# ScalarE and VectorE take the work of a query/key head in another order

## The chip, the cores and the metric

The kernel runs on one core of one Trainium2 chip. The metric is the device time of one execution in microseconds (us). Matmuls run on TensorE (PE in the profile, its weight loads PEld); elementwise work runs on ScalarE (ACT), VectorE (DVE) and GpSimd (POOL); SyncE (SP) issues most transfers. The engines run their own lists of instructions in order and wait for each other by semaphores.

## What is computed

A layer on x of 32 x 32 x 512: a channel mix chosen by condition, attention with 32 heads of 128 over sequences of 32, then a state space convolution and a feed-forward product with low-rank additions. The change touches the attention's query/key part alone:

```python
q = hidden_states @ Wq + bq
k = hidden_states @ Wk + bk
q = rms_norm(q, gq)      # over all 4096 columns: sums of squares over all heads
k = rms_norm(k, gk)
attn = einsum('bhqd,bhkd->bhqk', q, k) * scale   # then softmax, times v, times Wo
```

The 1024 tokens are the moving side of the products. The norms are applied to the scores later, so the head loop only adds up the squares of q and k.

## The kernel before

Each fp32 product is made of three fast matmuls: both sides are split into a high part (rounded) and a low part (the rest), and hi*hi, hi*lo and lo*hi are added in PSUM (L636 to L638). For the weights ScalarE makes `w_hi` by a copy (`split_hi`, L915) and VectorE makes `w_lo` by a subtraction (`split_lo`, L1141).

Queries and keys of a head are made together by a fast scheme with seven half products, p1 to p7, instead of eight, each 128 x 512 with two chunks of depth, six matmuls. The sums and differences of weight blocks that it needs are made by GpSimd (`combine`, L422: four operations, two heads ahead and more), and the sums of products by VectorE (`post`, L1193: `c11`, `u2`, `u4`, `c12`, `c22`, `u3`, `c21`), which reads PSUM and the tile `qk_sb`.

Weights and `qk_sb` have two slots, by the parity of the head. The query/key stage runs from some 24 us to 441 us of the span. The lists of a head h are written out by hand:

- TensorE, `head_qk` (L673): wait for `w_lo` of h; p1, p2; wait for `c21` of h-1; p6, p5, p3, p7; scores of h-1 (`head_scores`, L662, which waits for the scaled query, `c21` and for the scores of h-2 to be extracted, s_ok); wait for `u2` of h; p4. Each product also waits for its PSUM bank.
- ScalarE, `head` (L973): split of the next head's weights, blocks 0 to 4 (L981); key eviction of p1 with bias (L985), which releases `c11`; split of blocks 4 to 7 (L987); square of the key of h-1 (L971, behind `c21`); wait for `c12`; square of the query of h (L1000); scale of the query (L1003); extraction of the scores of h-1 (`extract`, L960, four instructions).
- VectorE, `head` (L1234): `c21` of h-1; `split_lo` of h+1 (L1144); `c11`, `u2`, `u4`; addition of the key squares of h-1 (L1232); `c12`, `c22`, `u3`; addition of the query squares of h (L1232).
- SyncE: the load of the weights of h+3 waits for `split_lo` of h+1 (`wlo_ok`), and so does GpSimd's `combine`.

Behind the last head the value stage starts: SyncE loads the first value weights `wv_raw` when p4 of head 30 is done (L312), ScalarE (L1017) and VectorE (`split_v`, L1270) split them, and TensorE makes value group 0, then the scores of head 31 (L748 to L752). `wv_raw` lies where `w_raw` of slot 0 lay, `wv_hi` where `w_hi` and part of `w_lo` of slot 0 lay.

Of the kernel before, what the change touches and what calls it, by code (L numbers as in the profile page):

```python
# [22 lines left out]
F32 = mybir.dt.float32  # L23
F32R = mybir.dt.float32r
I32 = mybir.dt.int32
ALU = mybir.AluOpType
ACT = mybir.ActivationFunctionType
# [5 lines left out]
HEADS, HD = 32, 128  # L33
INNER = HEADS * HD
KC = FEAT // P
# [26 lines left out]
def build_program(nc, x, cond_idx, lengths, cond_w, wq, bq, wk, bk, wv, bv, wo, bo, gq, gk,  # L62
# [3 lines left out]
    with ctx:  # L66
# [129 lines left out]
        ws_start, ws_ok, whi_ok, wlo_ok = (sem(n) for n in ("ws_start", "ws_ok", "whi_ok", "wlo_ok"))  # L196
# [63 lines left out]
        def _(sp):  # L260
# [48 lines left out]
                sp.wait_ge(wo_mm, t * G)  # L309
                load_o(t, wo_raw)  # L310

            sp.wait_ge(p4_mm, HEADS - 1)  # L312
            load_v(0)
            sp.wait_ge(p4_mm, HEADS)
            load_o(0, wo_raw)
# [574 lines left out]
        def _(act):  # L890
# [24 lines left out]
            def split_hi(slot, lo, hi):  # L915

                return sc.activation(w_hi[slot][:, lo:hi, :].rearrange("p b n -> p (b n)"),  # L917
                                     w_raw[slot][:, lo + 1:hi + 1, :].rearrange("p b n -> p (b n)"), ACT.Copy)
# [10 lines left out]
            for g in range(4):  # L929
                mix_out(g)  # L930
            act.wait_ge(ws_start, 4)
            split_hi(0, 0, 7).then_inc(whi_ok, 2)
            for g in range(4, G):
                mix_out(g)
            act.wait_ge(prm_mm, 1)
# [17 lines left out]
            def extract(h):  # L953


                act.wait_ge(s_mm, h + 1)
                dst = scores[:].rearrange("p h g k -> p (h g k)")[:, bass.ds(here(h) * (G * 32), G * 32)]
                for b in range(BPG):
                    src = bank(6, 1024)[quadrant(b), :].rearrange("p (g k) -> p g k", g=G)[:, :, quadrant(b)]
                    last = sc.activation(dst[quadrant(b), :].rearrange("p (g k) -> p g k", g=G), src, ACT.Copy)  # L960
                last.then_inc(s_ok, 1)

            def square_k(h, slot):
                act.wait_ge(c21_ok, h + 1)
                if isinstance(h, int) and h == 0:
                    out = sumsq[:, 1, :]
                else:
                    out = sq[:, 1, :]
                    if not (isinstance(h, int) and h == 1):
                        act.wait_ge(k_sum, h - 1)  # L970
                sc.activation(out, qk_sb[:, slot, 1, :], ACT.Square).then_inc(k_sq, 1)  # L971

            def head(h, slot, last_head=False):  # L973
                first = isinstance(h, int) and h == 0
                if not last_head:
                    if first:
                        act.wait_ge(ws_start, 8)
                    else:
                        act.wait_ge(ws_ok, h * 4)
                        act.wait_ge(p4_mm, h)  # L980
                    split_hi(1 - slot, 0, 4).then_inc(whi_ok, 1)  # L981
                act.wait_ge(p1_mm, h + 1)
                if not (isinstance(h, int) and h < 2):
                    act.wait_ge(s_mm, h - 1)
                sc.activation(qk_sb[:, slot, 1, halves(0)], bank(0), ACT.Identity, bias=bias("bk", h)).then_inc(p1_ok, 1)  # L985
                if not last_head:
                    split_hi(1 - slot, 4, 7).then_inc(whi_ok, 1)  # L987
                if first:
                    for n in range(4):
                        t_hi_out(n)  # L990
                else:
                    square_k(h - 1, 1 - slot)
                act.wait_ge(c11_ok, h + 1)
                act.wait_ge(c12_ok, h + 1)
                if first:
                    sc.activation(sumsq[:, 0, :], qk_sb[:, slot, 0, :], ACT.Square).then_inc(q_sq, 1)
                else:
                    if not (isinstance(h, int) and h < 2):
                        act.wait_ge(q_sum, h - 1)
                    sc.activation(sq[:, 0, :], qk_sb[:, slot, 0, :], ACT.Square).then_inc(q_sq, 1)  # L1000
                act.wait_ge(q_sq, h + 1)
                at = here(h)
                sc.activation(qk_sb[:, slot, 0, :], qk_sb[:, slot, 0, :], ACT.Copy,  # L1003
                              scale=gqk[:, bass.ds(at, 1)]).then_inc(q_ok, 1)
                if not first:
                    extract(h - 1)

            act.wait_ge(gqk_ok, 2)
            head(0, 0)
# [1 line left out]
            with act.Fori(1, HEADS // 2 - 1) as i:  # L1011
                for j in range(2):
                    head(i * 2 + j, j)
            head(HEADS - 2, 0)
            head(HEADS - 1, 1, last_head=True)
            act.wait_ge(wv_in, 16)
            sc.activation(wv_hi[:].rearrange("p c n -> p (c n)"), wv_raw[:].rearrange("p c n -> p (c n)"),  # L1017
                          ACT.Copy).then_inc(wvhi_ok, 1)
            square_k(HEADS - 1, 1)


            def value_out(t, g):
# [94 lines left out]
        def _(dve):  # L1117
# [22 lines left out]

            def split_lo(h, slot):  # L1141

                dve.wait_ge(whi_ok, h * 2 + 2)
                v.tensor_tensor(w_lo[slot][:].rearrange("p b n -> p (b n)"),  # L1144
                                w_raw[slot][:, 1:8, :].rearrange("p b n -> p (b n)"),
                                w_hi[slot][:].rearrange("p b n -> p (b n)").bitcast(F32), ALU.subtract).then_inc(wlo_ok, 1)
# [79 lines left out]
            def add_squares(m, h, done, total):  # L1226


                dve.wait_ge(done, h + 1)
                if not (isinstance(h, int) and h == 1):  # L1230
                    dve.wait_ge(total, h - 1)
                v.tensor_tensor(sumsq[:, m, :], sumsq[:, m, :], sq[:, m, :], ALU.add).then_inc(total, 1)  # L1232

            def head(h, slot, last_head=False):  # L1234
                first = isinstance(h, int) and h == 0
                if not first:
                    post("c21", h - 1, 1 - slot)
                    if not last_head:
                        dve.wait_ge(p4_mm, h)
                if not last_head:  # L1240
                    split_lo(h + 1, 1 - slot)
                post("c11", h, slot)
                post("u2", h, slot)
                post("u4", h, slot)
                if not first:
                    if not (isinstance(h, int) and h == 1):
                        add_squares(1, h - 1, k_sq, k_sum)
                post("c12", h, slot)
                post("c22", h, slot)
                post("u3", h, slot)  # L1250
                if not first:
                    add_squares(0, h, q_sq, q_sum)

            dve.wait_ge(gqk_ok, 2)
            head(0, 0)
# [7 lines left out]
                    head(i * 2 + j, j)  # L1263
            head(HEADS - 2, 0)

            def split_v(t, parts=(0, 1, 2, 3)):
                if 0 in parts:
                    dve.wait_ge(wvhi_ok, t + 1)
                for c in parts:
                    last = v.tensor_tensor(wv_lo[:, c, :], wv_raw[:, c, :], wv_hi[:, c, :].bitcast(F32), ALU.subtract)  # L1270
                if KC - 1 in parts:
                    last.then_inc(wvlo_ok, 1)

            head(HEADS - 1, 1, last_head=True)
            split_v(0)
            post("c21", HEADS - 1, 1)
            add_squares(1, HEADS - 1, k_sq, k_sum)


# [175 lines left out]
```

## Time and profile before

| | us |
|---|---|
| median of 3 runs | 950.04 (949.18 to 950.06) |
| the profiled execution | 949.06 |
| its span | 947.3 |
| TensorE busy | 877.5 (93%) |
| VectorE busy | 600.8 (63%) |
| ScalarE busy | 384.4 (41%) |
| GpSimd busy | 438.2 (46%) |

"Busy" is the time in which an engine had an instruction under way. TensorE's matmuls are pipelined and their ends are modelled: one of 512 columns is shown with 0.39 us while the next starts 0.23 us after it. So TensorE's work is read from the starts. The granted clock is the share of full speed (2.4 GHz) that TensorE had; its other level is 1.2 GHz.

### The profile page before, as it was taken

Reading aid. Unit: us, or ns where it says so; the run is one execution under the profiler, and the core shown is the slowest. Engines: PE = TensorE matmul, PEld = TensorE weight load, DVE = VectorE, ACT = ScalarE, POOL = GpSimd, SP = SyncE. Lnnn points to the kernel's source line nnn. Section 1 sums busy time; section 2 is a strip of 40 time slices with the busy share of each in tenths; the row PEclk is TensorE's granted clock in tenths of the full one; section 3 lists DMA queues with packets and bytes.
Section 4 is the critical chain, followed back from the end, with each engine's and each line's share of the span. In section 5 each row is a group of like instructions: output and inputs, shape, how many; then the busy total and the mean of one; then the engine's idle time right before and its main releaser. Section 6 shows DMA issues by size and latency. Waiting matters only on the chain.

```text
span 947.3 us, 12406 instructions
## 1 busy us (share of the span) xinstructions
PE 877.5 (93%) x4529; PEld 722.6 (76%) x4529; DVE 600.8 (63%) x650; ACT 384.4 (41%) x523; POOL 438.2 (46%) x401
## 2 busy tenths in 40 slices
PE   5698799999999999997889989999999999999998
PEld 4586588777777777776678868888888888888466
DVE  5974977777777777774775634677666765534431
ACT  3454455555555555554342342314142323222410
POOL 0888822223333333303999433699639990000500
PEclk9898999999999999998989989999999999999999
DMA  5142111111111111102001112411141111157402
GB/s 161 45 129 53 44 44 44 44 44 37 31 43 44 44 44 44 44 15 74 19 27 45 45 31 65 38 48 41 44 90 45 45 45 47 71 195 199 124 12 78
DMA packets 83570, 56.51 MB, mean 60 GB/s; under 512 B 33639, under 2 KB 66759, under 8 KB 83415
## 3 DMA queue, kind: packets, MB, share of 16 engines
q1 hardware_dynamic: 82576, 55.67, 20.3%
q10 hardware_dynamic: 966, 0.48, 0.2%
q8 instruction: 17, 0.28, 0.1%
q14 instruction: 11, 0.08, 0.0%
HBM read 52.32 MB, written 3.82 MB: 59 GB/s over the span
## 4 chain that ended last, share of the span: by engine, by line
PE 49%; ACT 3%; DVE 2%; issue 1%; DMA 1%; ACTq 0%; DVEq 0%
PE psum L590 13%; PE psum L591 13%; PE psum L592 13%; PE psum L729 5%; PE psum L833 1%; PE psum L862 1%; PE psum L884 1%; DMA wv_raw<-in_wv 1%; DVE wv_lo L1270 1%; PE psum L845 0%; PE psum L787 0%; ACT x2p L1098 0%; PE psum L805 0%; DVE wv_lo L1351 0%; ACT ang L1070 0%
## 5 line engine op out<-in xcount | busy, mean ns | idle before, releaser
L636 PE MATMUL psum<-t_hi,w_hi 128*128 128x512 f32 x256 | 107.6, 420 | 36.2 <-DVE qk_sb L1224 20.9
L1144 DVE TENSOR_TENSOR w_lo<-w_raw,w_hi 128x1792 fp32r<-128x1792 f32 x32 | 66.9, 2091 | 103.6 <-ACT w_hi L917 103.6
L430 POOL TENSOR_TENSOR w_raw<-w_raw 128x256 f32<-128x256 f32 x30 | 25.3, 842 | 199.5 <-DMA w_raw<-in_wk 199.3
L590 PE MATMUL psum<-wv_hi,mix_hi 128*128 128x512 f32 x256 | 102.6, 401 | 8.0 <-DVE wv_lo L1270 5.1
L637 PE MATMUL psum<-t_lo,w_hi 128*128 128x512 f32 x256 | 102.0, 398 | 0.0
L638 PE MATMUL psum<-t_hi,w_lo 128*128 128x512 f32 x256 | 101.6, 397 | 0.0
L591 PE MATMUL psum<-wv_lo,mix_hi 128*128 128x512 f32 x256 | 101.5, 397 | 0.0
L1360 DVE TENSOR_TENSOR acc<-psum,acc 128x512 f32<-128x512 f32 x64 | 44.2, 690 | 90.4 <-PE psum L592 90.2
L592 PE MATMUL psum<-wv_hi,mix_lo 128*128 128x512 f32 x256 | 101.4, 396 | 0.0
L1000 ACT ACTIVATE sq<-qk_sb 128x1024 f32<-128x1024 f32 x31 | 32.9, 1063 | 158.4 <-issue 154.3
L636 PEld LDWEIGHTS psum<-t_hi,w_hi 128*128 128x128 f32 x256 | 49.2, 192 | 56.1 <-DVE qk_sb L1224 31.0
L1036 ACT ACTIVATE attn_hi<-psum,params 128x512 fp32r<-128x512 f32 x64 | 43.7, 688 | 112.3 <-PE psum L729 111.8
L590 PE MATMUL psum<-wo_hi,attn_hi 128*128 128x512 f32 x224 | 87.4, 390 | 0.0
L591 PE MATMUL psum<-wo_lo,attn_hi 128*128 128x512 f32 x224 | 87.4, 390 | 0.0
L592 PE MATMUL psum<-wo_hi,attn_lo 128*128 128x512 f32 x224 | 87.2, 389 | 0.0
L1024 ACT ACTIVATE v_sb<-psum 128x512 f32<-128x512 f32 x64 | 38.1, 598 | 111.9 <-PE psum L592 111.4
L1232 DVE TENSOR_TENSOR sumsq<-sumsq,sq 128x1024 f32<-128x1024 f32 x62 | 80.2, 1294 | 1.1 <-ACT sq L971 1.1
L636 PE MATMUL psum<-mix_hi,w_hi 128*128 128x512 f32 x192 | 75.6, 394 | 1.7 <-ACT params L936 1.7
L637 PE MATMUL psum<-mix_lo,w_hi 128*128 128x512 f32 x192 | 75.4, 393 | 0.0
L638 PE MATMUL psum<-mix_hi,w_lo 128*128 128x512 f32 x192 | 75.2, 392 | 0.0
L729 PE MATMUL psum<-p_blocks,v_sb 128*128 128x128 f32 x512 | 60.8, 281 | 6.4 <-DVE p_blocks L1330 5.4
L917 ACT ACTIVATE w_hi<-w_raw 128x1024 fp32r<-128x1024 f32 (+2 forms) x63 | 60.5, 960 | 14.3 <-POOL w_raw L435 8.7
(233 smaller groups left out, 1958.0 us busy)
## 6 DMA issues: line engine op xcount, KB each, us to landing
w_raw<-in_wq SPq DMA_DIRECT2D x32, 256.0 KB, 2.9
w_raw<-in_wk SPq DMA_DIRECT2D x32, 256.0 KB, 3.2
wv_raw<-in_wv SPq DMA_DIRECT2D x8, 1024.0 KB, 5.4
toep<-kpad_dram SPq DMA_DIRECT2D x2, 4096.0 KB, 15.3
wo_raw<-in_wo SPq DMA_DIRECT2D x7, 1024.0 KB, 5.3
x_nat<-in_x SPq DMA_DIRECT2D x4, 512.0 KB, 5.9
acc<-in_x SPq DMA_DIRECT2D x1, 2048.0 KB, 10.0
out_dram<-o_stage SPq DMA_DIRECT2D x8, 256.0 KB, 2.0
```

Source lines behind the costliest of these rows:

```text
L590: mm(out, lh, rh, start=(n == 0), stop=False)
L591: mm(out, lh, rl, start=False, stop=False)
L592: last = mm(out, ll, rh, start=False, stop=(close and n == len(terms) - 1))
L636: mm(bank(n), wh, hi[:, c, tok], start=(i == 0), stop=False)
L637: mm(bank(n), wh, lo[:, c, tok], start=False, stop=False)
L638: last = mm(bank(n), wl, hi[:, c, tok], start=False, stop=(i == 1))
L729: last = mm(bank(2 + u % 4)[:, P * (g % 4):P * (g % 4) + P], v_sb[:, g, HD * h:HD * h + HD], p_blocks[:, h, g, :], start=True, stop=True)
L917: return sc.activation(w_hi[slot][:, lo:hi, :].rearrange("p b n -> p (b n)"), w_raw[slot][:, lo + 1:hi + 1, :].rearrange("p b n -> p (b n) ...
L1036: sc.activation(attn_hi[:, h, HALF * half:HALF * half + HALF], bank(2 + u % 4), ACT.Identity, bias=params[:, PARAM["bv"], bass.ds(at, 1)]) ...
L1144: v.tensor_tensor(w_lo[slot][:].rearrange("p b n -> p (b n)"), w_raw[slot][:, 1:8, :].rearrange("p b n -> p (b n)"), w_hi[slot][:].rearran ...
L1232: v.tensor_tensor(sumsq[:, m, :], sumsq[:, m, :], sq[:, m, :], ALU.add).then_inc(total, 1)
L1360: v.tensor_tensor(acc[:, g, :], bank(6 + g % 2), acc[:, g, :], ALU.add).then_inc(acc_ok, 1)
```

## The change

The lists of a head are put in another order on two engines.

- ScalarE: the split of the next head's weights becomes one instruction (blocks 0 to 7) and stands behind the square of the key of h-1, ahead of the wait for `c11` and `c12`. The extraction of the scores of h-2 stands at the head of head h's list, where the extraction of h-1 had stood at the end of h's list; the last one, extract(HEADS - 2), stands behind the last square. In the last head the split of `wv_raw` stands where the weights' split stands in the others, behind a wait for p4 of head 30.
- VectorE: the addition of query squares of h-1 stands behind `c21` of h-1; `split_lo` of h+1 stands behind `c12` of h; in the last head `split_v(0)` stands there.
- `whi_ok` counts one a head instead of two.
- SyncE: the load of `wv_raw` waits for `split_lo` of head 30 instead of p4 of head 30.

The diff, without the two places where `split_v` only moves in the text and the initial count of `whi_ok`:

```diff
@@ -309,7 +309,7 @@
                 sp.wait_ge(wo_mm, t * G)
                 load_o(t, wo_raw)
 
-            sp.wait_ge(p4_mm, HEADS - 1)
+            sp.wait_ge(wlo_ok, HEADS - 1)
             load_v(0)
             sp.wait_ge(p4_mm, HEADS)
             load_o(0, wo_raw)
@@ -970,26 +970,37 @@
                         act.wait_ge(k_sum, h - 1)
                 sc.activation(out, qk_sb[:, slot, 1, :], ACT.Square).then_inc(k_sq, 1)
 
+            def split_next(h, slot):
+
+                if isinstance(h, int) and h == 0:
+                    act.wait_ge(ws_start, 8)
+                else:
+                    act.wait_ge(ws_ok, h * 4)
+                    act.wait_ge(p4_mm, h)
+                split_hi(1 - slot, 0, 7).then_inc(whi_ok, 1)
+
+            def split_v0():
+
+                act.wait_ge(wv_in, 16)
+                act.wait_ge(p4_mm, HEADS - 1)
+                sc.activation(wv_hi[:].rearrange("p c n -> p (c n)"), wv_raw[:].rearrange("p c n -> p (c n)"),
+                              ACT.Copy).then_inc(wvhi_ok, 1)
+
             def head(h, slot, last_head=False):
                 first = isinstance(h, int) and h == 0
-                if not last_head:
-                    if first:
-                        act.wait_ge(ws_start, 8)
-                    else:
-                        act.wait_ge(ws_ok, h * 4)
-                        act.wait_ge(p4_mm, h)
-                    split_hi(1 - slot, 0, 4).then_inc(whi_ok, 1)
+                if not (isinstance(h, int) and h < 2):
+                    extract(h - 2)
                 act.wait_ge(p1_mm, h + 1)
-                if not (isinstance(h, int) and h < 2):
-                    act.wait_ge(s_mm, h - 1)
                 sc.activation(qk_sb[:, slot, 1, halves(0)], bank(0), ACT.Identity, bias=bias("bk", h)).then_inc(p1_ok, 1)
-                if not last_head:
-                    split_hi(1 - slot, 4, 7).then_inc(whi_ok, 1)
                 if first:
                     for n in range(4):
                         t_hi_out(n)
                 else:
                     square_k(h - 1, 1 - slot)
+                if last_head:
+                    split_v0()
+                else:
+                    split_next(h, slot)
                 act.wait_ge(c11_ok, h + 1)
                 act.wait_ge(c12_ok, h + 1)
                 if first:
@@ -1002,8 +1013,6 @@
                 at = here(h)
                 sc.activation(qk_sb[:, slot, 0, :], qk_sb[:, slot, 0, :], ACT.Copy,
                               scale=gqk[:, bass.ds(at, 1)]).then_inc(q_ok, 1)
-                if not first:
-                    extract(h - 1)
 
             act.wait_ge(gqk_ok, 2)
             head(0, 0)
@@ -1013,10 +1022,8 @@
                     head(i * 2 + j, j)
             head(HEADS - 2, 0)
             head(HEADS - 1, 1, last_head=True)
-            act.wait_ge(wv_in, 16)
-            sc.activation(wv_hi[:].rearrange("p c n -> p (c n)"), wv_raw[:].rearrange("p c n -> p (c n)"),
-                          ACT.Copy).then_inc(wvhi_ok, 1)
             square_k(HEADS - 1, 1)
+            extract(HEADS - 2)
 
 
             def value_out(t, g):
@@ -1140,7 +1147,7 @@
 
             def split_lo(h, slot):
 
-                dve.wait_ge(whi_ok, h * 2 + 2)
+                dve.wait_ge(whi_ok, h + 1)
                 v.tensor_tensor(w_lo[slot][:].rearrange("p b n -> p (b n)"),
                                 w_raw[slot][:, 1:8, :].rearrange("p b n -> p (b n)"),
                                 w_hi[slot][:].rearrange("p b n -> p (b n)").bitcast(F32), ALU.subtract).then_inc(wlo_ok, 1)
@@ -1231,14 +1238,20 @@
                     dve.wait_ge(total, h - 1)
                 v.tensor_tensor(sumsq[:, m, :], sumsq[:, m, :], sq[:, m, :], ALU.add).then_inc(total, 1)
 
...
             def head(h, slot, last_head=False):
                 first = isinstance(h, int) and h == 0
                 if not first:
                     post("c21", h - 1, 1 - slot)
-                    if not last_head:
-                        dve.wait_ge(p4_mm, h)
-                if not last_head:
-                    split_lo(h + 1, 1 - slot)
+                    if not (isinstance(h, int) and h == 1):
+                        add_squares(0, h - 1, q_sq, q_sum)
                 post("c11", h, slot)
                 post("u2", h, slot)
                 post("u4", h, slot)
@@ -1246,10 +1259,14 @@
                     if not (isinstance(h, int) and h == 1):
                         add_squares(1, h - 1, k_sq, k_sum)
                 post("c12", h, slot)
+                if last_head:
+                    split_v(0)
+                else:
+                    if not first:
+                        dve.wait_ge(p4_mm, h)
+                    split_lo(h + 1, 1 - slot)
                 post("c22", h, slot)
                 post("u3", h, slot)
-                if not first:
-                    add_squares(0, h, q_sq, q_sum)
 
             dve.wait_ge(gqk_ok, 2)
             head(0, 0)
@@ -1263,17 +1280,9 @@
                     head(i * 2 + j, j)
             head(HEADS - 2, 0)
 
...
             head(HEADS - 1, 1, last_head=True)
-            split_v(0)
             post("c21", HEADS - 1, 1)
+            add_squares(0, HEADS - 1, q_sq, q_sum)
             add_squares(1, HEADS - 1, k_sq, k_sum)
 
 
```

## Rows read from the trace of the kernel before

**Rows 1.** TensorE waits, whole span: us in total, times, longest.

```profile
PE psum L636 <- DVE qk_sb L1224: 20.9, 24, 4.3
PE psum L636 <- DVE qk_sb L1205: 7.9, 3, 4.6
...
PE psum L590 <- DVE wv_lo L1270: 5.1, 1, 5.1
```

**Rows 2.** Timeline, ScalarE, one head: start us, us, operation, idle before.

```profile
201.12 1.06 ACT L1000 ACTIVATE sq<-qk_sb 128x1024 f32<-128x1024 f32 x1 [5.10 <-issue]
202.34 1.15 ACT L1003 ACTIVATE qk_sb<-qk_sb,gqk 128x1024 f32<-128x1024 f32 x1
203.39 1.52 ACT L960 ACTIVATE scores<-psum 32x256 f32 x4
204.94 1.06 ACT L917 ACTIVATE w_hi<-w_raw 128x1024 fp32r<-128x1024 f32 x1
206.02 0.69 ACT L985 ACTIVATE qk_sb<-psum,params 128x512 f32<-128x512 f32 x1
...
207.34 1.05 ACT L971 ACTIVATE sq<-qk_sb 128x1024 f32<-128x1024 f32 x1
213.49 1.06 ACT L1000 ACTIVATE sq<-qk_sb 128x1024 f32<-128x1024 f32 x1 [5.10 <-issue]
```

**Rows 3.** Timeline, VectorE, the same head.

```profile
207.48 2.02 DVE L1144 TENSOR_TENSOR w_lo<-w_raw,w_hi 128x1792 fp32r<-128x1792 f32 x1 [3.21 <-ACT w_hi L917]
209.42 0.75 DVE L1201 SCALAR_TENSOR_TENSOR qk_sb<-psum,dqk,qk_sb 128x512 f32<-128x512 f32 x1
...
211.53 1.22 DVE L1232 TENSOR_TENSOR sumsq<-sumsq,sq 128x1024 f32<-128x1024 f32 x1
212.67 0.74 DVE L1213 SCALAR_TENSOR_TENSOR qk_sb<-psum,dqk,qk_sb 128x512 f32<-128x512 f32 x1
213.44 0.69 DVE L1217 TENSOR_TENSOR qk_sb<-psum,qk_sb 128x512 f32<-128x512 f32 x1
...
214.65 1.31 DVE L1232 TENSOR_TENSOR sumsq<-sumsq,sq 128x1024 f32<-128x1024 f32 x1
```

**Rows 4.** Timeline, TensorE, head 1: p1, its scores, the next p1.

```profile
43.98 0.40 PE L636 MATMUL psum<-mix_hi,w_hi 128*128 128x512 f32 x1
...
52.16 0.38 PE L669 MATMUL psum<-qk_sb 128*128 128x128 f32 x2
...
55.32 0.39 PE L636 MATMUL psum<-mix_hi,w_hi 128*128 128x512 f32 x1
```

**Rows 5.** Timeline, TensorE, VectorE: p1 (heads 6, 31) and a c21.

```profile
117.58 0.39 PE L636 MATMUL psum<-mix_hi,w_hi 128*128 128x512 f32 x1
...
117.85 0.69 DVE L1224 TENSOR_TENSOR qk_sb<-psum,qk_sb 128x512 f32<-128x512 f32 x1 [0.74 <-PE psum L638]
...
423.25 0.39 PE L636 MATMUL psum<-mix_hi,w_hi 128*128 128x512 f32 x1
```

**Rows 6.** Busy time by stretch, value stage: engines, granted clock, DMA share, GB/s.

```profile
600.00:700.00 100.00, 100.00 (x553) 85.61 (x552) 65.03 (x60) 27.73 (x37) 75.85 (x32) 1.00 0.21 53
```

**Rows 7.** Timeline, GpSimd and VectorE, start of the stage.

```profile
90.64 4.60 POOL L458 TENSOR_TENSOR acc<-acc,bo_rows 128x2048 f32<-128x2048 f32 x1
...
93.25 3.86 DVE L1144 TENSOR_TENSOR w_lo<-w_raw,w_hi 128x1792 fp32r<-128x1792 f32 x1 [6.34 <-ACT w_hi L917]
...
102.28 4.27 DVE L1232 TENSOR_TENSOR sumsq<-sumsq,sq 128x1024 f32<-128x1024 f32 x1
```

**Rows 8.** Timeline, TensorE, first value group and the scores behind it.

```profile
440.90 0.77 PE L590 MATMUL psum<-wv_hi,mix_hi 128*128 128x512 f32 x1 [5.08 <-DVE wv_lo L1270]
...
446.05 1.95 PE L669 MATMUL psum<-qk_sb 128*128 128x128 f32 x16
```

**Rows 9.** Page, transfers (KB each, us to landing); timeline, ScalarE, value split.

```profile
wv_raw<-in_wv SPq DMA_DIRECT2D x8, 1024.0 KB, 5.4
...
436.31 1.91 ACT L1017 ACTIVATE wv_hi<-wv_raw 128x2048 fp32r<-128x2048 f32 x1
```

More of the change, by code:

```diff
@@ L931, in _ @@
             act.wait_ge(ws_start, 4)
-            split_hi(0, 0, 7).then_inc(whi_ok, 2)
+            split_hi(0, 0, 7).then_inc(whi_ok, 1)
             for g in range(4, G):
@@ L1232, in add_squares, with split_v @@
                 v.tensor_tensor(sumsq[:, m, :], sumsq[:, m, :], sq[:, m, :], ALU.add).then_inc(total, 1)
+            def split_v(t, parts=(0, 1, 2, 3)):
+                if 0 in parts:
+                    dve.wait_ge(wvhi_ok, t + 1)
+                for c in parts:
+                    last = v.tensor_tensor(wv_lo[:, c, :], wv_raw[:, c, :], wv_hi[:, c, :].bitcast(F32), ALU.subtract)
+                if KC - 1 in parts:
+                    last.then_inc(wvlo_ok, 1)
             def head(h, slot, last_head=False):
@@ L1264, in _ @@
             head(HEADS - 2, 0)
[L1266 to L1272, printed above, removed]
             head(HEADS - 1, 1, last_head=True)
-            split_v(0)
             post("c21", HEADS - 1, 1)
+            add_squares(0, HEADS - 1, q_sq, q_sum)
             add_squares(1, HEADS - 1, k_sq, k_sum)
```

## Prediction

> **What bounds the kernel now.** I read the list of waits first, for TensorE: of its long idle times the largest total, 20.9 us in 24 pieces, ends with L1224, which is VectorE's `c21` of the query/key stage; another 7.9 us in 3 pieces ends with L1205, VectorE's `u2`, and 5.1 us with the first `wv_lo` at L1270 [rows 1]. TensorE has 93% of the span as busy time, so the question is what makes it wait in the heads.
>
> Then I read the timeline of one head on ScalarE and VectorE. ScalarE squares a query at 201.12 and the next one at 213.49: 12.37 us a head [rows 2]. Between them stands a closed ring in which each piece starts as the one before ends: square 201.12, scale 202.34, score extraction 203.39, first part of the weight split 204.94, key eviction (L985) 206.02 with the second part of the split behind it, VectorE's `split_lo` 207.48, `c11`, `u2`, `u4` from 209.42, the addition of key squares 211.53, `c12` 212.67, and again the square at 213.49 [rows 2, 3]. In this ring TensorE has no part.
>
> TensorE's own need is seen in head 1, where it did not wait: p1 starts at 43.98 and p1 of the next head at 55.32, so 11.34 us [rows 4]. The seven products take (52.16 - 43.98) / 6 = 1.36 us each for the six ahead of the scores, and scores with p4 take 55.32 - 52.16 = 3.16. So the stage is bound by the ring of the two other engines, and TensorE spends the difference of about 1.03 us a head on the wait ahead of p6. From p1 of head 6 (117.58) to p1 of head 31 (423.25) there are 25 heads in 305.67 us, 12.23 each; the first few of them still used up a lead [rows 5].
>
> **The change, part by part.** No arithmetic goes away; one ScalarE instruction a head does (two pieces of the split become one). The 1024-column piece takes 1.06 us [rows 2], so 1792 columns take at most 1.06 x 1.75 = 1.86 (an estimate).
>
> *The ring.* The weight split leaves the place ahead of L985, `split_lo` leaves the place ahead of `c11`, and the squares of the query are added behind `c21` and not ahead of it. The extraction moves in the text only: extract(h-1) at the head of the next head's list still follows the scale of head h at once. What is left of the ring: square 1.22, scale 1.05, extraction 1.55, L985 0.69, `c11`/`u2`/`u4` 2.11, key squares 1.14, `c12` 0.82 [rows 2, 3]. Sum 8.6 us, under 11.34. TensorE becomes the bound if nothing else is late, so I lay out a head of 11.34 with p1 at 0. A product's result is seen by VectorE 0.27 us behind the start of the next product (`c21` at 117.85, p1 at 117.58) [rows 5].
>
> VectorE: `c21` of the old head waits for p4, so from 0.27 and 0.69 long, then the query squares, 1.31, which end at about 2.2. `c11` waits for p2: 2.73 + 0.27 = 3.0. `u2` follows p6 at 4.4, `u4` follows p5 at 5.7, key squares 6.4 to 7.5, `c12` to 8.3, `split_lo` 2.02 to 10.3, then `c22` and `u3` (0.77 and 0.61, from the spacing 212.67, 213.44 and 214.65) to 11.7 [rows 3]. The next `c21` starts at 11.7 instead of 11.6 and ends at 12.4, where p6 needs it at 11.34 + 2.73 = 14.1. The new wait that matters is that p1 of the next head needs `split_lo`: ready at 10.3, wanted at 11.34, so 1.0 us of room where there had been some 4. VectorE is busy some 9 us a head, and its list has about 0.8 us of room before `c11`.
>
> ScalarE: L985 waits for p1 and starts at about 1.6, the key square (1.05) ends at 3.3, the whole split at 5.2, in time for 8.3. The query square follows `c12` at 8.3, the scale ends at 10.7, and the extraction, whose scores ended at 10.1, at 12.2, that is 0.9 of the next head, ahead of L985 at 1.6. All other semaphores of TensorE are early: scores(h-1) wants the scale and s_ok at 8.2 and has them at about -0.6 and 0.9. Queued behind `split_lo`'s wait on VectorE are `c22` and `u3`, needed by p7 and p6 only a head later.
>
> SyncE's loads of weights hang on `split_lo`, which is now late in a head; the load and GpSimd's sums for head h+3 are wanted three heads later by the split, so a load (some 3 us) and the sums (some 4) are hidden with two heads to spare. If that cover were gone, the whole of about 7 us would fall on each head.
>
> So 25 heads take 283.5 in place of 305.67: **22.2 us**. TensorE without a pause at full clock for 100 us is seen in the value stage, granted clock 1.00 [rows 6], so I charge no throttling.
>
> *The start of the stage (up to p1 of head 6).* Here GpSimd is late: between its weight sums it works on exponentials and adds the bias rows to `acc` (L458). The sums for head 5 are done when L458 starts, 90.64 [rows 7]. The split ends at 92.5, and `split_lo`, which had taken 3.86 us from 93.25 in place of 2.02, ends where it ended before, 97.1, because L458 runs until 95.24 [rows 7]. The row shows it: the two never run together. The Trainium skill, SBUF — State Buffer, section Who interferes with whom, says that an operation of VectorE with two inputs in SBUF and one of GpSimd that reads SBUF hold a common read port in turns, each to its end; the trace agrees (3.86 against 2.02). Without that rule p1 of head 5 would come at 94.5 and the sum would gain 2.6 us more.
>
> p1 of head 5 is then at 97.2 and p1 of head 6 at 108.5, or when `split_lo`(6) is done: key squares had ended at 102.28 + 4.27 = 106.55 behind the same GpSimd operation [rows 7], then `c12` and `split_lo`, 2.9, so 109.4. TensorE idles for some 6 us ahead of 97.2, and after such idle times it ran at half clock: the value group at 440.90 took 5.15 us until 446.05, where twelve matmuls take 2.73, a loss of 2.4 [rows 8]. I charge it: 108.5 + 2.4 = 110.9. Gain 117.58 - 110.9 = **6.7 us**, bounds 5 (if half clock lasts longer) and 8.2 (if it doesn't come).
>
> *The end of the stage.* The load of `wv_raw` waits for `split_lo`(30) in place of p4(30): about 12 us earlier, with a landing of 5.4 us [rows 9]. Its split takes 1.91 on ScalarE [rows 9] and is behind the key square: 3.3 to 5.2 of head 31, and VectorE's half (about 2.5) ends at 10.8, before p4 ends. So the value group starts 11.34 behind p1(31), where it was 440.90 - 423.25 = 17.65: **6.3 us**. Its half clock goes with the idle time: **2.4 us**. Against it stands extract(30), now behind the last key square: `c21`(31) ends at 12.3, key square 13.4, extraction 14.9; the last scores want it at 14.1 with the value group done: **-1.0 us** (0 to -1.6).
>
> *Behind it* the same chains (norm, softmax, GpSimd's tables) start from the same points and move as a whole; 0, with 2 either way.
>
> Sum: 22.2 + 6.7 + 6.3 + 2.4 - 1.0 = 36.6 us. The profiled execution took 949.06 (span 947.3 with 1.8 around it), 0.1% under the median of 950.04. 949.06 - 36.6 = **912.5 us**, -3.9%.
>
> **The rivals.**
> *A. A second ring takes over part of it.* p1(h) to `c12`(h) to `split_lo`(h+1) to p1(h+1) closes at 10.3. If operations of both engines lengthen each other (a blocked `split_lo` took 3.86, so +1.84 [rows 7]), it closes at 12.1 and 25 heads give nothing more than 3 us. For it: VectorE has two more pairs of SBUF inputs in a row. Against it: GpSimd's sums start some 3.8 us behind the end of `split_lo`, when VectorE works from PSUM. Half of that, 11.2, costs nothing; the full amount gives 912.5 + 19 = 932.
> *B. Slower than before.* The same gate, one mechanism: `split_lo` waits behind `c12`, so each head's first product hangs on the end of the VectorE list. It costs more than the whole gain if the ring closes above 12.23 + 14.4 / 25 = 12.8 us, 2.5 over what I count, as when blocking (1.84) meets each head together with a late `u4`. At 13.2 the time is 949.06 + 10 = 959.
> *C. It doesn't do what it says:* the room is used up by another wait and TensorE's idle time only moves from p6 to p1. Then the stage keeps 12.23, only the end gains its 7.7 and the start perhaps 1: 940. For no change at all, both must be lost too.
> *D. The clock.* The Trainium skill, TensorE: Matmul & The Clock Gate, section HAM oscillation, says that idle gaps throttle the array. By rows, one more stretch of half clock costs 2.4 us or somewhat more: 915 to 917. It stays in the forecast's own range.
>
> **How the numbers follow.** Forecast with D 0.80 (906 to 920), A 0.10 (920 to 935), C 0.05 (935 to 948), no difference 0.02, B 0.03. Four fifths are held by 906 to 922: the lower end takes the start and the end at their best and a shorter head (11.3), the upper end some of A. A measurement of this kernel tells 0.2% from no change. Faster 0.95, same 0.02, slower 0.03.
>
> **What would show it.** The square L1000 every 11.3 us instead of 12.37; no TensorE wait on L1224 in the middle heads; `split_lo` behind `c12`, ending about 1 us ahead of p1; the value group directly behind p4(31), and a wait of 1 us ahead of the last scores, ended by the extraction; `split_lo` near 97 us still long. It is wrong if TensorE's waits reappear ended by L1144.

## The result and the profile after

| | before | after |
|---|---|---|
| median of 4 executions, us | 949.63 | 912.9 (912.25 to 914.61) |
| the profiled execution | 949.06 | 912.63 |
| its span | 947.3 | 910.8 |
| TensorE busy | 877.5 (93%) | 865.6 (95%) |
| VectorE busy | 600.8 (63%) | 592.7 (65%) |
| ScalarE busy | 384.4 (41%) | 378.3 (42%) |
| GpSimd busy | 438.2 (46%) | 418.8 (46%) |

The ratio is 0.9616, with a 95% interval of 0.9599 to 0.9633: 36.7 us less by the medians, 36.5 by the spans of the two profiled executions.

The waits of TensorE over the whole span of the changed kernel, as in [rows 1]: us in total, times, longest.

```profile
PE psum L636 <- DVE w_lo L1151: 10.1, 3, 6.1
...
PE psum L729 <- DVE p_blocks L1339: 4.5, 1, 4.5
...
PE psum L669 <- ACT scores L960: 1.0, 1, 1.0
```

The 24 waits on `c21` are gone, and so are those on `u2` and on the first `wv_lo`. New are three on `split_lo` (now L1151), all at the start of the stage (1.6, 2.4 and 6.1 us, ahead of p1 of heads 1, 4 and 5), and one of 1.0 us on the extraction of scores.

One head on ScalarE in the changed kernel, the same view as [rows 2]:

```profile
201.25 1.06 ACT L1011 ACTIVATE sq<-qk_sb 128x1024 f32<-128x1024 f32 x1 [3.37 <-issue]
202.46 1.15 ACT L1014 ACTIVATE qk_sb<-qk_sb,gqk 128x1024 f32<-128x1024 f32 x1
203.51 1.52 ACT L960 ACTIVATE scores<-psum 32x256 f32 x4
205.97 0.69 ACT L994 ACTIVATE qk_sb<-psum,params 128x512 f32<-128x512 f32 x1 [0.94 <-PE psum L638]
206.56 1.05 ACT L971 ACTIVATE sq<-qk_sb 128x1024 f32<-128x1024 f32 x1
207.51 1.69 ACT L917 ACTIVATE w_hi<-w_raw 128x1792 fp32r<-128x1792 f32 x1
212.57 1.06 ACT L1011 ACTIVATE sq<-qk_sb 128x1024 f32<-128x1024 f32 x1 [3.37 <-issue]
```

From square to square it is 11.32 us, not 12.37. The key eviction (now L994) no longer starts where the piece ahead of it ends: it waits 0.94 us for TensorE's p1. The ring is open.

The same head on VectorE, as [rows 3]:

```profile
204.56 0.69 DVE L1231 TENSOR_TENSOR qk_sb<-psum,qk_sb 128x512 f32<-128x512 f32 x1 [0.26 <-PE psum L638]
205.17 1.22 DVE L1239 TENSOR_TENSOR sumsq<-sumsq,sq 128x1024 f32<-128x1024 f32 x1
207.38 0.75 DVE L1208 SCALAR_TENSOR_TENSOR qk_sb<-psum,dqk,qk_sb 128x512 f32<-128x512 f32 x1 [0.99 <-PE psum L638]
208.64 0.69 DVE L1212 TENSOR_TENSOR qk_sb<-psum,qk_sb 128x512 f32<-128x512 f32 x1 [0.51 <-PE psum L638]
210.00 0.69 DVE L1216 TENSOR_TENSOR qk_sb<-psum,qk_sb 128x512 f32<-128x512 f32 x1 [0.67 <-PE psum L638]
210.61 1.22 DVE L1239 TENSOR_TENSOR sumsq<-sumsq,sq 128x1024 f32<-128x1024 f32 x1
211.74 0.74 DVE L1220 SCALAR_TENSOR_TENSOR qk_sb<-psum,dqk,qk_sb 128x512 f32<-128x512 f32 x1
212.40 2.02 DVE L1151 TENSOR_TENSOR w_lo<-w_raw,w_hi 128x1792 fp32r<-128x1792 f32 x1
```

`c21`, `c11`, `u2` and `u4` now each wait for TensorE, 0.26 to 0.99 us. Behind `u4` key squares, `c12` and `split_lo` stand back to back until 214.42, and TensorE starts the next p1 at 215.61:

```profile
113.73 0.39 PE L636 MATMUL psum<-mix_hi,w_hi 128*128 128x512 f32 x1
...
204.29 0.39 PE L636 MATMUL psum<-mix_hi,w_hi 128*128 128x512 f32 x1
...
215.61 0.39 PE L636 MATMUL psum<-mix_hi,w_hi 128*128 128x512 f32 x1
...
396.73 0.39 PE L636 MATMUL psum<-mix_hi,w_hi 128*128 128x512 f32 x1
```

These are p1 of heads 6, 14, 15 and 31. From head 6 to head 31 it is 283.00 us, where it was 305.67 [rows 5]: 11.32 a head. The busy time by stretch over these 25 heads, before (PE, PEld, VectorE, ScalarE, GpSimd; granted clock; DMA share; GB/s):

```profile
117.60:423.20 305.60, 289.75 (x1451) 240.02 (x1450) 221.33 (x247) 172.99 (x246) 86.77 (x93) 1.00 0.13 39
```

and after:

```profile
113.70:396.70 283.00, 283.00 (x1451) 241.81 (x1450) 222.56 (x251) 171.33 (x228) 70.23 (x96) 1.00 0.16 48
```

1451 matmuls in both and a full clock in both; after, TensorE is busy all of the 283.00 us.

### The profile page after: what moved, and what is told of

Same layout as the page of the kernel before. It is cut to its first block, busy times and chain, and to the rows that moved or that the text cites. A ratio compares the mean times of both kernels' runs of the same rounds, so it can differ in the third digit from the quotient of the medians.

```text
span 910.8 us, 12373 instructions
## 1 busy us (share of the span) xinstructions
PE 865.6 (95%) x4529; PEld 721.2 (79%) x4529; DVE 592.7 (65%) x650; ACT 378.3 (42%) x492; POOL 418.8 (46%) x401
## 4 chain that ended last, share of the span: by engine, by line
PE 85%; POOL 4%; DVE 4%; ACT 3%; DMA 1%; issue 1%; ACTq 0%; SPq 0%; POOLq 0%; DVEq 0%
PE psum L590 13%; PE psum L591 13%; PE psum L592 13%; PE psum L636 10%; PE psum L637 10%; PE psum L638 10%; PE psum L729 6%; PE psum L669 5%; PE psum L833 2%; PE psum L862 1%; DVE w_lo L1151 1%; PE psum L884 1%; PE psum L612 1%; POOL small L450 1%; DMA wv_raw<-in_wv 1%
## 5 line engine op out<-in xcount | busy, mean ns | idle before, releaser
L636 PE MATMUL psum<-t_hi,w_hi 128*128 128x512 f32 x256 | 103.5, 404 | 7.3 <-DVE t_lo L1197 7.3
L1239 DVE TENSOR_TENSOR sumsq<-sumsq,sq 128x1024 f32<-128x1024 f32 x62 | 76.3, 1231 | 0.0
L1151 DVE TENSOR_TENSOR w_lo<-w_raw,w_hi 128x1792 fp32r<-128x1792 f32 x32 | 67.1, 2097 | 8.9 <-ACT w_hi L917 8.9
L729 PEld LDWEIGHTS psum<-p_blocks,v_sb 128*128 128x128 f32 x512 | 60.9, 199 | 5.8 <-issue 4.9
L669 PEld LDWEIGHTS psum<-qk_sb 128*128 128x128 f32 x512 | 62.0, 191 | 3.8 <-issue 1.4
## 6 DMA issues: line engine op xcount, KB each, us to landing
acc<-in_x SPq DMA_DIRECT2D x1, 2048.0 KB, 10.7
```

Source lines behind the costliest of these rows:

```text
L636: mm(bank(n), wh, hi[:, c, tok], start=(i == 0), stop=False)
L669: last = mm(bank(6, 1024)[:, P * g:P * g + P], qk_sb[:, slot, 0, P * g:P * g + P], qk_sb[:, slot, 1, P * g:P * g + P], start=True, stop=True)
L729: last = mm(bank(2 + u % 4)[:, P * (g % 4):P * (g % 4) + P], v_sb[:, g, HD * h:HD * h + HD], p_blocks[:, h, g, :], start=True, stop=True)
```

## The experiments

Each is an edit of the changed kernel and was run several times beside the kernel before. The kernel before had a median of 949.2 to 949.4 us there. The changed kernel was run once more among the last ones:

> The changed kernel itself on the same chip as the three others: 913, ratio 0.9616 to the kernel before, and a half-clock stretch more or less (1.7 us each) as the spread between its executions.

Measured: 912.96 us (ratio 0.9617, 0.9601 to 0.9633). Against it the medians below are read; 0.2% of it is 1.8 us.

### Which of the moves opens the ring

**ScalarE's split back in two pieces and in the old places** (`split_next` then splits blocks 0 to 4 only, and `whi_ok` counts two a head again; not shown):

```diff
                 if not (isinstance(h, int) and h < 2):
                     extract(h - 2)
+                if not last_head:
+                    split_next(h, slot)
                 act.wait_ge(p1_mm, h + 1)
                 sc.activation(... bank(0), ACT.Identity, bias=bias("bk", h)).then_inc(p1_ok, 1)
+                if not last_head:
+                    split_hi(1 - slot, 4, 7).then_inc(whi_ok, 1)
...
-                else:
-                    split_next(h, slot)
```

> The changed kernel with the weight split of ScalarE back in its two old pieces and places (blocks 0 to 4 ahead of the key eviction, 4 to 7 behind it). Theory V (VectorE's order alone opens the ring): the ring from c12 to c12 then holds square 1.22, scale 1.05, extraction 1.55, split 1.08, eviction 0.6, c11 to u4 2.11, key squares 1.14, c12 0.82, sum 9.6 us, under TensorE's 11.32; time 913, within 0.3% of the changed kernel. Rival S (ScalarE's order carries the gain): the key eviction is late again, the heads go back to 12.2 us or more, time 935 to 945.

Measured: 914.35 us, ratio 0.9631 (0.9615 to 0.9647), p1 to p1 of 11.32 us in all middle heads. ScalarE's order carries 1.4 us at most, which a measurement hardly tells from nothing. By the traces it is nothing: p1 of head 31 starts at 397.38, against 397.48 in the changed kernel run again, and 1.5 us more lie at the very end (95.9 us from the last wait on `wv_lo` on, not 94.4, with a granted clock of 0.96 and not 0.98).

**`split_lo` back ahead of `c11`, ScalarE as changed:**

```diff
+                if not last_head:
+                    if not first:
+                        dve.wait_ge(p4_mm, h)
+                    split_lo(h + 1, 1 - slot)
                 post("c11", h, slot)
...
                 post("c12", h, slot)
                 if last_head:
                     split_v(0)
-                else:
-                    if not first:
-                        dve.wait_ge(p4_mm, h)
-                    split_lo(h + 1, 1 - slot)
```

> The changed kernel with split_lo back ahead of c11, ScalarE as changed. Theory V: the ring closes over both splits and the key square as well: 1.22 + 1.05 + 1.55 + 0.60 + 0.95 + 1.61 + 1.94 + 2.11 + 1.14 + 0.82 = 13.0 us a head, slower than the kernel before in the heads; 25 x 1.7 = 42 us more than the changed kernel, 950 to 960. Rival S: ScalarE's order keeps most of the gain, under 930.

Measured: 959.75 us, ratio 1.0114 (1.0096 to 1.0132): 47 us over the changed kernel and slower than the kernel before; heads of 13.07 to 13.11. ScalarE and VectorE in one head of it, the split and what stands behind it:

```profile
199.60 1.69 ACT L917 ACTIVATE w_hi<-w_raw 128x1792 fp32r<-128x1792 f32 x1
207.34 1.06 ACT L1011 ACTIVATE sq<-qk_sb 128x1024 f32<-128x1024 f32 x1 [6.04 <-issue]
```

```profile
201.32 2.02 DVE L1151 TENSOR_TENSOR w_lo<-w_raw,w_hi 128x1792 fp32r<-128x1792 f32 x1 [3.85 <-ACT w_hi L917]
203.27 0.74 DVE L1208 SCALAR_TENSOR_TENSOR qk_sb<-psum,dqk,qk_sb 128x512 f32<-128x512 f32 x1
```

`split_lo` waits 3.85 us for the whole split, which itself stands behind the key square now, and the chain goes on over `c11` to the query square at 207.34. ScalarE's half of the change without the move of `split_lo` is a loss, though this kernel keeps the query squares and the end of the stage as changed; VectorE's half without ScalarE's, again with the end as changed, gives all but 1.4 us of the gain.

**The query squares back ahead of `c21`:** `add_squares(0, h, ...)` stands behind `u3` again.

> The changed kernel with the addition of the query squares back in its old place (behind u3, ahead of c21). By the measured offsets c21 would then end some 1.2 us later, at 2.1 us behind p4 in place of 0.95, where p6 needs it at 2.73: no change, 913, heads of 11.32. Rival (c21 behind the additions was the wait that TensorE stood in): waits on c21 ahead of p6 return, 0.3 us or more a head, 920 and above.

Measured: 915.3 us, ratio 0.9644 (0.9628 to 0.966). The heads stay at 11.32, so this wait was none of TensorE's as long as the ring is open. Of the 2.3 us, 1.0 is seen at the end of the stage: the scores of head 31 wait 1.99 us for the extraction, not 0.99, as `c21` and the last key square are later. Another 1.2 is TensorE's clock: behind the wait of 2.90 us at 525.09 the granted clock of the 12 us from 524 on is 0.72, where it is 0.86 in the changed kernel, and the stretch from there to the next wait takes 293.65 us, not 292.4. No run moves `split_lo` and nothing else; that the other two moves are not needed is shown for each by itself, here and above.

**All orders inside the heads as before, the change around the last head kept** (the three edits together):

> Both engines' orders inside the heads as before (two split pieces, split_lo ahead of c11, query squares ahead of c21); kept is only the change around the last head: value weights loaded behind split_lo(30), their split inside head 31, extract(30) behind the last key square. My sum gives this part 6.3 + 2.4 - 1.0 = 7.7 us: 942, heads of 12.3. Rival: the end gives nothing of its own, 949; or more, if what followed the value group also gained from it, 939.

Measured: 942.18 us (seven executions, 939.16 to 946.90), ratio 0.9929 (0.9902 to 0.9956), heads of 12.2 to 12.5. By the medians the end is worth 7.2 us by itself, 7.7 by the sum; the interval allows 4 to 9. The steps agree less well than the totals: the first value group starts 12.4 us behind p1 of head 31, so 5.2 of the 6.3 are there; it takes 4.87 us until the last scores, where it took 5.15, so 0.3 of the 1.4, as the scores wait 1.99 us for the extraction; and 1.0 more comes behind them, where I had put 0.

**The load of the first value weights behind p4(30) again:**

```diff
-            sp.wait_ge(wlo_ok, HEADS - 1)
+            sp.wait_ge(p4_mm, HEADS - 1)
             load_v(0)
```

> The changed kernel with the load of the first value weights waiting for p4 of head 30 again, the rest as changed. p4(30) ends at about 397 of the changed kernel's span; issue 0.4 and landing 5.5 bring the weights at 402.8, ScalarE's split 1.9 ends at 404.7, and VectorE reaches its half at 404.84 anyway. Theory O (the order around the last head carries the 6.3 us, the earlier load nothing): 913, within 0.3% of the changed kernel. Rival L (the earlier load carries it): the value group starts 5 us later and at half clock, 918 to 921.

Measured: 912.98 us, ratio 0.9625 (0.9599 to 0.9651), value group 11.32 behind p1(31). The earlier load gives nothing; the place of the value split in the lists does it.

### How much room the new gate has

`split_lo` now stands right ahead of the first product that needs it. To measure the room, part of `w_lo` is worked out twice, ahead of the full `split_lo`, in one kernel 768 columns and in the other all 1792:

```diff
                 dve.wait_ge(whi_ok, h + 1)
+                v.tensor_tensor(w_lo[slot][:, 0:3, :]..., w_raw[slot][:, 1:4, :]...,
+                                w_hi[slot][:, 0:3, :]..., ALU.subtract).then_inc(again, 1)
+                dve.wait_ge(again, h + 1)
                 v.tensor_tensor(w_lo[slot][:]..., w_raw[slot][:, 1:8, :]..., w_hi[slot][:]..., ALU.subtract)
```

> The changed kernel with 768 columns of w_lo worked out twice, ahead of each split_lo: about 0.87 us more on VectorE behind c12 (by 2.02 us for 1792 columns). The room behind split_lo is 215.61 - 214.42 = 1.2 us in the changed kernel, so the heads stay at 11.32 and the time at 913 to 916. Rival (the gate of split_lo has no real room, since blocking by GpSimd uses it up): heads of 11.6 and more, 921 and above.

Measured: 925.24 us, ratio 0.9742 (0.9726 to 0.9758), heads of 11.65 to 11.80. This I had wrong: the room is smaller than I read it. One head of this kernel on GpSimd, VectorE and TensorE:

```profile
252.81 0.73 POOL L436 TENSOR_TENSOR w_raw<-w_raw 128x256 f32<-128x256 f32 x1
```

```profile
252.41 0.69 DVE L1221 TENSOR_TENSOR qk_sb<-psum,qk_sb 128x512 f32<-128x512 f32 x1 [0.67 <-PE psum L639]
253.02 1.60 DVE L1244 TENSOR_TENSOR sumsq<-sumsq,sq 128x1024 f32<-128x1024 f32 x1
254.55 0.74 DVE L1225 SCALAR_TENSOR_TENSOR qk_sb<-psum,dqk,qk_sb 128x512 f32<-128x512 f32 x1
255.21 0.94 DVE L1152 TENSOR_TENSOR w_lo<-w_raw,w_hi 128x768 fp32r<-128x768 f32 x1
256.18 2.02 DVE L1156 TENSOR_TENSOR w_lo<-w_raw,w_hi 128x1792 fp32r<-128x1792 f32 x1
```

```profile
258.26 0.50 PE L637 MATMUL psum<-mix_hi,w_hi 128*128 128x512 f32 x1
```

From `u4` to the end of `split_lo` it is 258.20 - 252.41 = 5.79 us; in the changed kernel 214.42 - 210.00 = 4.42. Of the 1.37 more, 0.97 is the added operation. The other 0.4 is the key squares: 1.60 us, not 1.22. GpSimd's last sum (252.81, 0.73) is still under way when they start at 253.02. The load of weights hangs on `split_lo`, the sums on the load, so a later `split_lo` pushes the sums into the key squares. In the changed kernel they miss each other by 0.5 us. From p1 to `u4` it is 5.84 us in this head (5.71 in the changed kernel), and from the end of `split_lo` to p1 0.06: together 11.69, the head as measured.

> The changed kernel with all 1792 columns of w_lo worked out twice: 1.93 us more. Behind the room of 1.2 us, 0.75 us a head are left over: heads of 12.1, 25 x 0.75 = 19 us, with the others some 21 to 24 more, 933 to 938, and TensorE's idle time ends with split_lo ahead of p1. Rival (VectorE's list is short of time as a whole and not by this gate): heads of 11.3 still, as VectorE's busy time of 9.1 + 1.9 = 11.0 us is under 11.32; 914.

Measured: 960.52 us, ratio 1.0114 (1.0092 to 1.0135), over 20 us above my range: heads of 12.62 to 12.88, not 12.1, with TensorE waiting 1.1 to 1.2 us for `split_lo` ahead of each p1. The wait ends where I said. The 2.0 added and the 0.4 of blocking (key squares of 1.53 and 1.59 us here as well), less a room of 1.0, make 1.4 a head, as measured. VectorE's list is not full; it is the gate. The time is 11 us above the kernel before at heads of 12.7, where rival B had put the turning point at 12.8: it had left out that the start loses as well (p1 of head 6 at 126.10, 12 us later than in the changed kernel).

### The start of the stage, and a faster version

**GpSimd's sums of heads 4 to 9 each stand two heads earlier in its list:**

```diff
             combine(3, 1, 64)
+            combine(4, 0, 96)
             exp_in_place(sm("ea"), sm("t0"), sm("t1"))
+            combine(5, 1, 96)
...
-            combine(4, 0, 96)
+            combine(6, 0, 128)
             exp_in_place(sm("ex"), sm("t0"), sm("t1"))
-            combine(5, 1, 96)
+            combine(7, 1, 128)
...
             for n in range(2):
+                combine(8 + n, n, 160)
                 gp.tensor_tensor(acc[:, 4 * n:4 * n + 4, :], ...).then_inc(acc_set, 1)
-                combine(6 + n, n, 128)
-            with pool.Fori(4, HEADS // 2) as i:
+            with pool.Fori(5, HEADS // 2) as i:
```

> The changed kernel with GpSimd's list put in another order at the start of the stage: the weight sums of heads 4 to 9 each stand two heads earlier against the exponentials and the bias additions to acc, which come later. Theory G (the start is bound by GpSimd's late sums, 2.4 + 6.1 us of idle TensorE ahead of p1 of heads 4 and 5 and 2.6 us of half clock behind them): 912.9 - 9 to 11 = 902 to 904. Rival (the idle time only moves, since the exponentials then meet the sums of the later heads): 908 to 913.

Measured: 907.31 us (903.53 to 911.84), ratio 0.9557 (0.9516 to 0.9598). p1 of head 6 is at 100.97, 12.8 us earlier, but ahead of p1 of head 8 a new wait of 5.57 us stands, with half clock behind it. GpSimd, VectorE and TensorE there:

```profile
122.92 4.52 POOL L461 TENSOR_TENSOR acc<-acc,bo_rows 128x2048 f32<-128x2048 f32 x1
```

```profile
122.94 6.38 DVE L1153 TENSOR_TENSOR w_lo<-w_raw,w_hi 128x1792 fp32r<-128x1792 f32 x1
```

```profile
129.38 0.80 PE L638 MATMUL psum<-mix_hi,w_hi 128*128 128x512 f32 x1 [5.57 <-DVE w_lo L1153]
```

`split_lo` starts 0.02 us behind a bias addition of 4.52 us and takes 6.38: that length and its own 1.9. The time lies between the two ranges, and the rival held in part: the time of the sums was won, and some of it was lost again, to the long additions and not to the exponentials as the rival had it.

**The same, with the two bias additions cut into eight, one behind the sums of each of heads 8 to 15** (the lines taken out, and VectorE's wait for eight of `acc_set` and not two, are not shown):

```diff
+            for g in range(G):
+                combine(8 + g, g % 2, (8 + g) // 2 * 32 + 32)
+                gp.tensor_tensor(acc[:, g, :], acc[:, g, :], bo_rows[:], ALU.add).then_inc(acc_set, 1)
+            with pool.Fori(8, HEADS // 2) as i:
```

> GpSimd's sums first, as before, and the two bias additions of 4.6 us each as eight of some 1.2 us, one behind each of the sums of heads 8 to 15. Theory P (one long GpSimd operation with SBUF inputs holds up split_lo for its whole length, 6.38 us where it takes 2.02): the idle time of 5.57 us ahead of p1 of head 8 and the half clock behind it go, heads of 11.32 from head 1 on, p1(31) at 384; 908.1 - 8.3 = 900. Rival: the pieces block split_lo or the key squares in eight heads by up to 1.2 us each, past the room of 1.0: 902 to 906.

Measured: 900.83 us (900.62 to 901.39), ratio 0.9491 (0.9475 to 0.9507). Heads of 11.32 to 11.45 from head 1 on, p1(31) at 385.46, and no wait of TensorE within them. This is the fastest version, 12.1 us under the changed kernel and 5.1% under the kernel before: 5.6 us by the sums moved forward, 6.5 by the pieces.

**extract(30) ahead of the last key square:** the two lines change places.

> The changed kernel with extract(30) ahead of the last key square and not behind it. The scores of head 31 waited 0.99 us for it at 411.92 (1.0 was my charge): it now ends at about 408.7, before the value group does at 410.8, so 1.0 us is gained: 912. Rival: the key square, 1.5 us later, makes the sums of squares late, nothing gained: 913.

Measured: 913.25 us, ratio 0.9631 (0.9612 to 0.965): nothing. The wait ahead of the last scores is gone, but not its microsecond. The waits of TensorE in this kernel, as above, and an operation that is longer, on VectorE, with GpSimd beside it:

```profile
PE psum L729 <- DVE p_blocks L1339: 5.7, 1, 5.7
PE psum L590 <- ACT v_sb L1031: 3.8, 2, 2.9
```

```profile
419.43 2.22 DVE L1296 SCALAR_TENSOR_TENSOR inv_norm<-var_k,var_q 128x256 f32<-128x256 f32 x1
```

```profile
418.58 2.78 POOL L479 TENSOR_TENSOR expo<-mult,small 128x1536 f32<-128x1536 f32 x1
```

The first `attend` waits 5.7 us for the softmax, not 4.5 (L1335, the scaling by `row_inv`, takes 2.36 us here and 1.23 in the changed kernel), and one value group 0.9 for an eviction. L1296 takes 2.22 us here and 0.97 in the changed kernel, and the traces say why: it ends 0.3 us behind GpSimd's L479 in both. L479 ends at 421.36 here and L1296 at 421.65; in the changed kernel L479 runs from 418.39 to 421.17 and L1296 from 420.48 to 421.45. In the kernel with both edits below it is the same again (409.63 and 409.91). GpSimd's list follows the last `c21`, which this edit doesn't move, so whatever reaches L1296 earlier waits there: the microsecond is lost to an operation of GpSimd.

> Both of the two: 1.0 us under the kernel with the pieces alone, 899. Rival as there.

Measured, both together: 902.77 us (899.38 to 903.85), ratio 0.9516 (0.95 to 0.9533), no better than the pieces alone. The profiled execution was the fastest of the four, at 899.38.

## Why the prediction was right, point by point

912.5 was forecast and 912.9 measured. The main term, the heads, is right for the reason given; that the total agrees to 0.4 us is luck, since the start gave 2.8 us too little and the part behind the stage 2.4 too much. By the steps of the sum, all from starts on TensorE (us):

| step | before | after | forecast | measured |
|---|---|---|---|---|
| up to p1 of head 6 | 117.58 | 113.73 | 6.7 | 3.9 |
| 25 heads, p1(6) to p1(31) | 305.67 | 283.00 | 22.2 | 22.7 |
| p1(31) to the first value group | 17.65 | 11.32 | 6.3 | 6.3 |
| value group to the last scores | 5.15 | 3.87 | 1.4 | 1.3 |
| from there to the end | 501.2 | 498.9 | 0 | 2.4 |
| sum | | | 36.6 | 36.5 |

**The heads and the ring.** Right in mechanism and in size. The ring of 12.37 was closed by `split_lo` ahead of `c11` (back there: 13.09, by its sum 13.0), and with it moved TensorE's own 11.32 is left. My sign of being wrong, waits of TensorE on this `split_lo`, did come, but in no middle head: only the three at the start. That only VectorE's place matters was my reading behind the result; the prediction had treated both moves together.

**The start.** Two terms miss and make up for each other, and this is the first: 6.7 was 2.8 too much, below my lower bound of 5. The step that failed is "the sums for head 5 are done when L458 starts, 90.64": I took GpSimd's list as it stood in the trace of before, and had called its loads and sums hidden. In the changed kernel, GpSimd (two views), VectorE and TensorE show:

```profile
49.02 0.74 POOL L430 TENSOR_TENSOR w_raw<-w_raw 128x256 f32<-128x256 f32 x1 [1.57 <-DMA w_raw<-in_wk]
...
53.59 2.17 POOL L411 TENSOR_SCALAR small<-small 128x32 f32<-128x32 f32 x1
...
74.77 1.73 POOL L431 TENSOR_TENSOR w_raw<-w_raw 128x256 f32<-128x256 f32 x1
...
93.24 4.51 POOL L458 TENSOR_TENSOR acc<-acc,bo_rows 128x2048 f32<-128x2048 f32 x1
```

```profile
53.59 2.02 DVE L1151 TENSOR_TENSOR w_lo<-w_raw,w_hi 128x1792 fp32r<-128x1792 f32 x1
...
95.04 4.59 DVE L1151 TENSOR_TENSOR w_lo<-w_raw,w_hi 128x1792 fp32r<-128x1792 f32 x1 [4.71 <-ACT w_hi L917]
```

```profile
81.95 0.50 PE L636 MATMUL psum<-mix_hi,w_hi 128*128 128x512 f32 x1 [2.41 <-DVE w_lo L1151]
...
99.69 0.79 PE L636 MATMUL psum<-mix_hi,w_hi 128*128 128x512 f32 x1 [6.12 <-DVE w_lo L1151]
```

The sums for head 5 are done at 93.24, 2.6 us later. At 53.59 a step of the exponential starts with `split_lo` and takes 2.17 us, where its like take 0.29; at 74.77 a sum takes 1.73, not 0.74. Each was held by an operation of VectorE with two inputs in SBUF that the new order had put beside it. But the kernel before has such pieces too, at other places, and the sum at 74.77 was not held there:

```profile
48.63 2.58 POOL L433 TENSOR_TENSOR w_raw<-w_raw 128x256 f32<-128x256 f32 x1
...
72.97 0.73 POOL L431 TENSOR_TENSOR w_raw<-w_raw 128x256 f32<-128x256 f32 x1
```

So the whole list has to be added up, from 39 us to the end of the sums for head 5. Before, eight operations are held, some 10.7 us together; after, nine, some 11.5. That is 0.8 of the 2.6 us. The list stands 0.3 later when this starts. The largest part, 1.57, is the wait at 49.02 for the weights of head 3: their load follows `split_lo` of head 1, which now stands behind `c12`, and is issued at 45.24 and not at 41.01.

So the hold-up that I charged in one direction (`split_lo` held by L458: here 4.59 us from 95.04) acts in the other as well. The idle time of 6.12 us and the half clock behind it (first matmul 0.79) came as charged.

**The end.** 6.3 by place of the value split, not by the earlier load, as the run with the late load shows. The half clock ahead of the last scores is gone, and the wait on the extraction came with 0.99 us where 1.0 was charged:

```profile
409.29 1.06 ACT L971 ACTIVATE sq<-qk_sb 128x1024 f32<-128x1024 f32 x1 [2.04 <-DVE qk_sb L1231]
410.26 1.52 ACT L960 ACTIVATE scores<-psum 32x256 f32<-32x256 f32 x4
```

```profile
408.05 0.39 PE L590 MATMUL psum<-wv_hi,mix_hi 128*128 128x512 f32 x1
...
411.92 0.80 PE L669 MATMUL psum<-qk_sb 128*128 128x128 f32 x5 [0.99 <-ACT scores L960]
```

The run with the extraction first shows that this wait is covered: without it the same time is spent at L1296, behind GpSimd's L479.

**Behind the stage.** I had said 0, 2 either way; it was 2.4, just outside. The reason I gave, that all chains behind the stage move as a whole, failed. By starts 0.8 us of it lie between the last scores and the first `attend` (29.92 before, 29.16 after), 0.2 from there to the next long wait, 1.3 from that to the one behind it (293.68 and 292.40), and 0.1 at the end. The 0.8 is on VectorE: its softmax chain meets GpSimd's tables at other points, and its scaling by `row_inv`, for one, takes 2.35 us before and 1.23 after. The 1.3 is TensorE's clock. Behind the same wait of 2.9 us for an eviction, at 559.21 before and 524.13 after, the stretches of 12 us read, before:

```profile
558.00:570.00 12.00, 10.79 (x35) 8.62 (x36) 8.43 (x8) 2.24 (x4) 9.83 (x28) 0.72 0.28 89
```

and after:

```profile
523.00:535.00 12.00, 10.87 (x41) 8.80 (x42) 9.10 (x9) 2.83 (x5) 9.83 (x28) 0.86 0.28 89
```

A granted clock of 0.72 is 2 x 0.28 x 12 = 6.7 us at 1.2 GHz, one of 0.86 is 3.4. Half of the difference would be 1.7 us saved; by the starts it is 1.3. The same wait stands ahead of both, so why it was shorter is open.

**The rivals.** A and B had the right mechanism with the wrong distance to it: the gate's room is 1.0 us, as laid out, but an operation that lengthens it also moves GpSimd's sums into the key squares, 0.4 more. The changed kernel is on the right side by little. C did not come. D is in the ledger with the one stretch charged and the one half as long.

## What to carry to other kernels

When the busiest engine stops a little in each turn of a loop, follow one turn from an instruction to itself on the other engines: if each piece starts as the one before ends and the sum is the period, take out of that ring the piece that nobody in it needs, and check which engine's list closes it, as here only one of two moves did the work. The moved piece has a new deadline; its room is to be read with what hangs on its end (the load, the sums, and which operations of other engines they then meet), not from its own length alone. And a gain ahead of a stage that is held by another engine's list is not read off that list as it was, since the list itself shifts with its neighbours and with the loads that hang on them.

## What the runs showed of the hardware that was not expected

One GpSimd operation with SBUF inputs holds up a VectorE operation with two SBUF inputs for its whole length: 6.38 us for a `split_lo` of 2.02 behind an addition of 4.52. In the other direction a GpSimd operation of 0.29 us took 2.17. A start earlier by 0.01 us decides which of the two is held: with VectorE's L1335 at 434.73 and GpSimd's L491 at 434.74, in the changed kernel, they take 1.23 and 2.35 us; at 434.92 and 434.91, with the extraction first, 2.36 and 1.29. Cutting two additions of 4.6 us into eight, with the sums moved forward, was worth 12 us. And the half-clock stretch behind one and the same wait of 2.9 us was 6.7 us long in the kernel before and 3.4 in the changed one, and in the fastest version it didn't come at all (granted clock 1.00 from 512 to 524 us, wait at 512.81); the time from this wait to the next was 293.7, 292.4 and 290.9 us.
